# Vision tower on one core: the opening loads in another order, position tables built by the host, and a new planned order of tasks

## The chip, the cores and the metric

The kernel runs on one core of a Trainium2 chip. Its engines are TensorE (PE: matrix products and transposes), VectorE (DVE), ScalarE (ACT), GpSimd (POOL) and SyncE (SP, which here only issues transfers and waits). The metric is the device time of one execution in microseconds; it was measured in three runs.

## The reference

The input is 32 images of 3 x 96 x 96 and 31 small parameter arrays. All is fp32. In short:

```
h = patches(x) as 36 rows of 768 per image               # tokenizer
h = layernorm(h, ln1) @ W + bias;  h = layernorm(h, ln2) + sincos positions
h = [cls_tok ; cls_token + cls_pos_embedding ; h]        # 38 rows of 256 per image, 1216 rows
h += causal 16-head attention(layernorm(h)), weights quantised to 5 levels:
     s = mean|w|;  w = clip(round(w / s), -2, 2) * s
h += tanh(layernorm(h) @ weight.T @ aux1.T @ aux2 + bias)
h += 16-head attention(layernorm(h)) with biases and a head mask
h += top-1 of 16 experts(layernorm(h)), hidden size 1024, 76 rows of room for each expert
```

## The kernel before

**Tiles.** A tile is three images (TROWS = 114 rows; 11 tiles, the last of 76). The tokens are kept in `tokens` (whose first 256 columns are `h`). Attention works on pairs of images (16 per layer). The raw patches come twice: `in_xt` by token, from which VectorE takes the mean and variance of each row (task `xs`), and `in_xf` by feature, the left side of the token product (task `tok`). Both come in five groups of tiles, XGROUPS = (0,1), (1,2), (2,4), (4,7), (7,11). The normalisation of the first layer norm is folded into the weights: `cs` (on PE, L742) sums the weighted columns of W and VectorE builds `tokWg` from it (L1080); `bs` adds up the bias (L748, L1087). `asum` (L1091) sums the absolute attention weights, PE adds them over the partitions (`qs`, L755), and VectorE quantises `attn0` (`qs`, L1096 to L1108). `fB` and `fW` (L766) multiply the three weights of the feed-forward layer into one; `wo` and `bo` do the head mask and a bias of the second attention layer. A tile's product goes through VectorE (`tok`, L1125), its variance through GpSimd (L654, L655: add epsilon, power -0.5), then `tokn` (L1134, L1135) applies the second norm and adds the table `addA`. GpSimd makes `addA` at the start (L637, L638) from three tables.

**PSUM.** Products that pass through the three banks `G` are numbered in PE's order (`uses`), and use n waits until use n - 3 has been emptied by VectorE or ScalarE.

**Values.** In each attention layer the value rows of a tile are copied to three blocks of partitions by 9 transfers on SP (`sp` task `v`, L599), after which GpSimd masks them by head (`vb`, L675). GpSimd also masks the keys (`km`, L662). Once the last token tile is done, SP issues the first expert weights, one piece after each `v`. After attention the rows are scattered to the experts (L695) into `expert_in`, which was first filled from `k_empty`, and the experts run in a loop (L919, L932).

**The order.** Each engine takes its tasks strictly in the order that `plan()` (L300) works out at build time. `needs()` gives the dependences, COST the planned time of each task, ARRIVES and XARRIVES the planned landing times of loads, HANDOVER what passing a result on costs, and GOAL the wanted times. At each step an engine picks, of the next tasks of its kinds, the one with the lowest value of

```
c[0] * EAGER + wanted(*c[1][1:])
```

where c[0] is the planned start (L340). The kernel's loads are issued at the start, on SP's queue (L560 to L571) and on ScalarE's (L953 to L960), each queue in the order of its lines. ScalarE's first task, and the first `tokn`, wait for `tables_ready` (L640).

## Time and profile before

| | |
|---|---|
| median of 3 runs | 445.86 us (443.11 to 446.62) |
| profiled execution | 444.86 us |
| its span | 443.2 us |
| mean granted TensorE clock | 0.892 of full |
| PE busy | 370.4 us (84%) |
| VectorE busy | 235.5 us (53%) |
| GpSimd busy | 178.0 us (40%) |
| ScalarE busy | 113.7 us (26%) |
| moved by DMA | 64.68 MB, mean 146 GB/s |

Times inside the span are counted from the first instruction. Busy time does not hold the issue of transfers, semaphore waits or branches; a matmul of the source is two or more records, since fp32 goes through in parts. Idle time of an engine counts only where something on the chain waits for it. The DMA engines are fully busy for about the first 40 us (296 to 429 GB/s in the page's slices of 11 us) and lightly used until the expert weights.

### The profile page before, as it was taken

The page shows a single profiled execution, that of the slowest core. Times are in us where ns is not written, and L with a number is a line of the kernel's source. Part 1 is how long each engine was busy: PE and PEld are TensorE (multiplying, and loading weights), DVE is VectorE, ACT ScalarE, POOL GpSimd, SP SyncE. Part 2 cuts the span into 40 slices and gives each one's busy share as a digit, 9 for nine tenths or more (in the row PEclk, how much of TensorE's full clock was granted, in tenths as well). Part 3 has the DMA queues.
Part 4 walks back from the last instruction along what each step waited for, and adds up shares of the span by engine and source line. Part 5 has one row for each costly group of instructions (what it writes and reads, how often), then busy time and mean ns, then how long its engine had stood idle before and what let it go on. Part 6 is the DMA issues. An engine that isn't in the chain of part 4 may idle for free.

```text
span 443.2 us, 9050 instructions
## 1 busy us (share of the span) xinstructions
PE 370.4 (84%) x3164; PEld 307.6 (69%) x3164; DVE 235.5 (53%) x675; ACT 113.7 (26%) x333; POOL 178.0 (40%) x264
## 2 busy tenths in 40 slices
PE   4649998799998989887858667984499999999992
PEld 3537886687787968766747546764398888888881
DVE  1298998687887368565666474465022232222221
ACT  0001233344444445343423322211021101111010
POOL 0224566665556537344536451645011313132221
PEclk9968999899999989888997895555589999999998
DMA  8997011110122212223233323531868999999200
GB/s 296 401 429 299 23 42 33 35 46 30 34 82 91 60 55 84 87 73 88 75 105 85 112 76 103 138 124 32 211 214 275 317 317 324 315 315 324 66 16 5
DMA packets 39237, 64.68 MB, mean 146 GB/s; under 512 B 5147, under 2 KB 30684, under 8 KB 38368
## 3 DMA queue, kind: packets, MB, share of 16 engines
q1 hardware_dynamic: 32752, 53.86, 36.7%
q10 hardware_dynamic: 2208, 6.82, 4.4%
q0 software_dynamic: 4240, 3.51, 3.0%
q8 instruction: 23, 0.38, 0.3%
q14 instruction: 14, 0.11, 0.1%
HBM read 53.20 MB, written 7.62 MB: 137 GB/s over the span
## 4 chain that ended last, share of the span: by engine, by line
PE 59%; issue 12%; DMA 8%; DVE 7%; SPq 6%; POOL 5%; ACT 1%; ACTq 1%; DVEq 0%; POOLq 0%
PE bank L919 13%; PE bank L932 12%; SPq L599 6%; PE bank L782 5%; PE bank L806 5%; PE bank L867 4%; DMA early<-in_xt 4%; PE bank L853 4%; PE bank L816 3%; DMA v<-vt 3%; PE bank L842 3%; PE bank L834 2%; PE bank L874 2%; POOL mid L662 2%; PE bank L791 1%
## 5 line engine op out<-in xcount | busy, mean ns | idle before, releaser
L675 POOL TENSOR_TENSOR mid<-v,tab 114x512 f32<-114x512 f32 x32 | 34.4, 1078 | 74.8 <-DMA v<-vt 51.9
L919 PEld LDWEIGHTS bank<-mid,early 128*128 128x128 f32 x512 | 61.9, 199 | 1.2
L919 PE MATMUL bank<-mid,early 128*128 (+1 forms) x512 | 61.9, 281 | 0.0
L932 PE MATMUL bank<-early,mid 128*76 128x256 f32 x256 | 57.9, 379 | 0.0
L853 PE MATMUL bank<-mid 114*38 114x51 f32 (+3 forms) x768 | 31.7, 232 | 21.2 <-issue 18.8
L853 PEld LDWEIGHTS bank<-mid 114*38 114x38 f32 (+1 forms) x768 | 28.8, 141 | 27.3 <-issue 25.2
L932 PEld LDWEIGHTS bank<-early,mid 128*76 128x76 f32 x256 | 36.6, 147 | 15.4
L712 POOL DMA_DIRECT2D mid<-in_b x14 | 7.9, 563 | 84.0 <-DVE idx L1228 84.0
L662 POOL TENSOR_TENSOR mid<-mid,tab 128x608 f32<-128x608 f32 x32 | 38.5, 1209 | 1.9 <-PE bank L834 1.8
L655 POOL TENSOR_TENSOR rs<-rs,mhalf 114x1 f32<-114x1 f32 (+4 forms) x60 | 36.8, 613 | 5.0
L806 PE MATMUL bank<-xnT,attn 128*128 128x228 f32 (+1 forms) x192 | 38.4, 355 | 0.0
L1032 ACT ACTIVATE mid<-bank,cols 128x76 f32<-128x76 f32 x64 | 15.5, 325 | 86.2 <-PE bank L919 86.2
L1216 DVE TENSOR_SCALAR mid<-bank,cols 128x76 f32<-128x76 f32 x64 | 14.5, 289 | 42.9 <-PE bank L919 42.9
L806 PEld LDWEIGHTS bank<-xnT,attn 128*128 128x128 f32 x192 | 35.1, 197 | 1.5 <-issue 0.4
L998 ACT COPY mid<-bank 114x612 f32<-114x612 f32 x32 | 21.4, 670 | 44.1 <-PE bank L842 44.1
L782 PE MATMUL bank<-early 128*114 128x256 f32 (+1 forms) x132 | 32.1, 400 | 0.4 <-DVE fv L1169 0.4
L654 POOL TENSOR_SCALAR rs<-mv 114x1 f32<-114x1 f32 (+4 forms) x60 | 15.2, 253 | 41.5 <-DVE mv L1055 29.9
L1149 DVE TENSOR_REDUCE mx<-bank 102x16 f32<-102x608 f32 x32 | 25.0, 783 | 12.6 <-PE bank L834 12.5
L867 PE MATMUL bank<-attn,mid 128*114 128x256 f32 (+1 forms) x88 | 29.3, 464 | 0.6 <-ACT mid L1003 0.4
L1144 DVE TENSOR_SCALAR xn<-tokens,mv,rs 114x256 f32<-114x256 f32 (+1 forms) x33 | 21.0, 644 | 16.5 <-POOL rs L655 15.6
L993 ACT ACTIVATE mid<-mid 102x608 f32<-102x608 f32 x32 | 22.8, 714 | 26.2 <-DVE mid L1152 26.0
L782 PEld LDWEIGHTS bank<-early 128*114 128x114 f32 (+1 forms) x132 | 24.3, 187 | 6.7 <-DVE fv L1169 0.8
(112 smaller groups left out, 588.9 us busy)
## 6 DMA issues: line engine op xcount, KB each, us to landing
early<-in_w SPq DMA_DIRECT2D x64, 512.0 KB, 5.1
v<-vt SPq DMA_DIRECT2D x192, 38.0 KB
expert_in<-k_empty SPq DMA_DIRECT2D x1, 2570.0 KB, 37.0
attn<-in_attn SPq DMA_DIRECT2D x2, 1024.0 KB, 19.5
early<-in_xt ACTq DMA_DIRECT2D x1, 1536.0 KB, 35.9
early<-in_xf SPq DMA_DIRECT2D x1, 1368.0 KB, 20.1
mid<-expert_in SPq DMA_DIRECT2D x8, 160.6 KB, 6.6
mid<-expert_in ACTq DMA_DIRECT2D x8, 160.6 KB, 7.0
```

What stands on the lines that cost most here:

```text
L599: sp.dma_start(v3[j * SEQ:(j + 1) * SEQ, (TILE_IMGS * n + a) % (2 * TILE_IMGS), :], vt[a * SEQ:(a + 1) * SEQ, (m - 1) % 2, :]).then_inc(v_ ...
L655: eng.tensor_tensor(rs[0:r, at, :], rs[0:r, at, :], bc(mhalf[0:r, :], 1, width), ALU.pow).then_inc(rs_ready, 1)
L662: eng.tensor_tensor(km[:, n % 2], bc(kT[:, :, n * PCOLS:(n + 1) * PCOLS], 2, 4), bc(bc(quarterm[:, :], 2, PCOLS), 1, KC), ALU.mult).then_i ...
L675: eng.tensor_tensor(Vb[0:TROWS, (m - 1) % 3, :, :, 0:HD], v3[:, at:at + 2, :].rearrange("p a (h d) -> p a h d", h=HEADS), bc(bc(blockm[:, ...
L782: mm_ = mm(ps[0:rows(n), 0:DIM], xT[:, n, j, 0:rows(n)], tokWg[:, j, :], start=j == 0, stop=j == PC - 1)
L806: ins = mm(ps[:, oc * width:(oc + 1) * width], w[:, kc, j * DIM + oc * 128:j * DIM + oc * 128 + 128], xnT[:, kc, gcols(n)], start=kc == 0, ...
L853: ins = mm(Op[r0:r1, h0 * VW:h1 * VW], PTs[0:TROWS, n % 2, j, r0:r1], Vb[0:TROWS, (m - 1) % 3, a, h0:h1, :], start=True, stop=True)
L867: ins = mm(ps[0:rows(n), 0:DIM], OT[:, kc, cols(n)], w[:, kc, :], start=kc == 0, stop=kc == KC - 1)
L919: ins = mm(Hp[b][:, c // 4, (c % 4) * ECOLS:(c % 4 + 1) * ECOLS], w1s[s][:, kc, c * 128:c * 128 + 128], xeT[:, bass.ds(it * SLOTS + s, 1), ...
L932: ins = mm(Yp[b][0:CAP, 0:DIM], hT[:, b, c, :], w2s[s][:, c, :], start=c == 0, stop=c == HC - 1)
L993: eng.activation(P[0:PROWS, n % 2], P[0:PROWS, n % 2], ACT.Exp).then_inc(p_exp, 1)
L1149: link(eng.tensor_reduce(mxv, sv, AX.X, ALU.max))
```

## The change

Four things are changed.

1. The sincos positions leave the constant table `k_tab` (553 columns become 297) and are put by the host into the second half of `in_table`, which held only the class position. GpSimd makes `addA` in one addition instead of two chained ones, into a tile of its own.
2. That addition, the scaling of `bq` and the copy of the row ids are no longer GpSimd's first work but a task `tabs`, placed by the planner. The first `tokn` depends on it in the plan; the waits in the kernel are as before.
3. The loads are issued in another order. SP: W, features 0, features 1, attn0, features 2, 3, 4, ffn0, attn1. ScalarE: cols, tokens 0, table, tokens 1, live, gain, tab, tokens 2, mask, tokens 3, tokens 4, k_empty. The mask and k_empty pass from SP's queue to ScalarE's.
4. The planner's arrivals, wanted times, TILE and EAGER have new values, so the order of the tasks on all engines is planned anew. COST is the same but for the new task.

```diff
--- before.py
+++ after.py
@@ -63,7 +63,7 @@
 NEG = -1.0e30
 DROP = 65536.0
 
-TAB = {"ident": 128, "head": 8, "quarter": 4, "block": HEADS, "upto": TROWS, "iota": EXP, "ids": TILES, "pos": DIM}
+TAB = {"ident": 128, "head": 8, "quarter": 4, "block": HEADS, "upto": TROWS, "iota": EXP, "ids": TILES}
 COLS = {"g1": PC, "be1": PC, "bq": KC, "bk": KC, "bv": KC, "gate": KC * EXP, "b1": EXP * HC}
 LIVE_ROWS = ["L0_tok_bias", "L0_ffn_bias", "L1_attn_bo", "L1_ffn_bg", "L1_attn_head_mask"]
 
...
@@ -115,6 +109,16 @@
     return np.ascontiguousarray(w.reshape(-1, 128, w.shape[-1]).transpose(1, 0, 2).reshape(128, -1))
 
 
+def positions():
+
+    omega = np.arange(DIM // 4, dtype=np.float32) / np.float32(DIM // 4 - 1)
+    omega = (np.float32(1.0) / np.power(np.float32(10000.0), omega)).astype(np.float32)
+    y, x = np.meshgrid(np.arange(HP, dtype=np.float32), np.arange(HP, dtype=np.float32), indexing="ij")
+    y, x = y.reshape(-1)[:, None] * omega, x.reshape(-1)[:, None] * omega
+    one = np.concatenate([np.zeros((2, DIM), np.float32), np.concatenate([np.sin(x), np.cos(x), np.sin(y), np.cos(y)], 1)], 0)
+    return one.astype(np.float32)
+
+
...
@@ -126,11 +130,12 @@
     by_feature = tok.reshape(TILES, TROWS, PC, 128).transpose(3, 0, 2, 1)
     row = lambda names: np.concatenate([inputs[n].reshape(1, -1) for n in names], 1)
     column = lambda name, k: inputs[name].reshape(k, 128).T
-    gain, add, cls_pos = [np.zeros((XROWS, DIM), np.float32) for _ in range(3)]
+    gain, add, place = [np.zeros((XROWS, DIM), np.float32) for _ in range(3)]
     for a in range(TILE_IMGS):
         at = a * SEQ
         gain[at + 2:at + SEQ], add[at + 2:at + SEQ] = inputs["L0_tok_ln2_g"].reshape(1, -1), inputs["L0_tok_ln2_b"].reshape(1, -1)
-        add[at], add[at + 1], cls_pos[at + 1] = inputs["cls_tok"].reshape(-1), inputs["L0_tok_cls_token"].reshape(-1), inputs["L0_tok_cls_pos_embedding"].reshape(-1)
+        place[at:at + SEQ] = positions()
+        add[at], add[at + 1], place[at + 1] = inputs["cls_tok"].reshape(-1), inputs["L0_tok_cls_token"].reshape(-1), inputs["L0_tok_cls_pos_embedding"].reshape(-1)
...
@@ -145,7 +150,7 @@
         "in_cols": np.ascontiguousarray(np.concatenate([
             column("L0_tok_ln1_g", PC), column("L0_tok_ln1_b", PC), qk_bias("L1_attn_bq"), qk_bias("L1_attn_bk"), column("L1_attn_bv", KC),
             by_rows(inputs["L1_ffn_Wg"]), inputs["L1_ffn_b1"].reshape(EXP * HC, 128).T], 1)),
-        "in_live": row(LIVE_ROWS), "in_gain": gain, "in_table": np.concatenate([add, cls_pos], 1),
+        "in_live": row(LIVE_ROWS), "in_gain": gain, "in_table": np.concatenate([add, place], 1),
...
@@ -169,26 +174,26 @@
     return v.to_broadcast(shape)
 
 
-PAIR, TILE, LAYER, EAGER = 7.41, 13.22, 126.9, 529.73
-
-GOAL = {"xs": -80.1, "cs": -215.9, "bs": -113.4, "asum": -20.1, "qs": -171.8, "fB": -118.7, "fW": 6.3, "wo": 51.3, "bo": 9.8,
-        "tok": -66.3, "tokn": -11.2, "lns0": -52.5, "lnt0": -41.6, "qk0": -35.7, "v": -4.5, "km": -49.3, "s": -0.2, "vb": 8.1, "pt": 8.7,
-        "pv": 15.8, "ot": 19.9, "proj": 28.5, "lns1": -74.7, "lnt1": 31.5, "ffn": 42.8, "ffnr": 30.3, "lns2": -36.9, "lnt2": 54.0,
-        "qk1": 66.1, "lns3": 30.6, "lnt3": 40.2, "log": 20.5, "cnt": 26.2, "scat": 79.9}
+PAIR, TILE, LAYER, EAGER = 7.41, 13.24, 126.9, 895.91
+
+GOAL = {"xs": -73.3, "tabs": -83.3, "cs": -201.3, "bs": -78.2, "asum": -29.1, "qs": -145.2, "fB": -132.3, "fW": 13.9, "wo": 34.6,
+        "bo": 4.2, "tok": -74.4, "tokn": -17.7, "lns0": -61.1, "lnt0": -43.3, "qk0": -34.7, "v": -5.2, "km": -99.7, "s": 1.2, "vb": 2.0,
+        "pt": 9.6, "pv": 16.5, "ot": 19.7, "proj": 28.4, "lns1": -88.6, "lnt1": 35.0, "ffn": 42.8, "ffnr": -2.7, "lns2": -95.3,
+        "lnt2": 57.3, "qk1": 69.2, "lns3": 24.1, "lnt3": 35.0, "log": 5.3, "cnt": -2.7, "scat": 64.7}
 
...
+        "pool": {"xs": 0.95, "tabs": 1.3, "tok": 0.9, "lns": 0.9, "km": 1.33, "vb": 1.12, "lnx": 0.78, "cnt": 0.36, "scat": 1.3},
...
-ARRIVES = {("pe", "cs"): 6.0, ("pe", "bs"): 6.0, ("dve", "asum"): 10.0, ("dve", "wo"): 25.0, ("pe", "fB"): 22.0}
-
-XARRIVES = [8.5, 11.0, 15.0, 20.0, 26.0]
+ARRIVES = {("pe", "cs"): 6.2, ("pe", "bs"): 6.2, ("dve", "asum"): 14.5, ("pool", "tabs"): 13.0, ("dve", "bs"): 11.0, ("dve", "wo"): 38.0, ("pe", "fB"): 34.0}
+
+XARRIVES = [8.9, 11.5, 17.0, 22.5, 30.0]
 
...
@@ -214,6 +219,7 @@
         step("pe", kind, 0, 0)
         step(EMPTIES[kind], kind, 0, 0, ("pe", kind, 0, 0))
     step("dve", "asum", 0, 0)
+    step("pool", "tabs", 0, 0)
     step("dve", "wo", 0, 0)
     after[("pe", "qs", 0, 0)] = [("dve", "asum", 0, 0)]
     after[("pe", "fW", 0, 0)] = [("act", "fB", 0, 0)]
@@ -226,7 +232,7 @@
         step("pe", "tok", 0, t, ("dve", "cs", 0, 0))
         step("dve", "tok", 0, t, ("pe", "tok", 0, t), ("pool", "xs", 0, group), ("dve", "bs", 0, 0))
         step("pool", "tok", 0, t, ("dve", "tok", 0, t))
-        step("dve", "tokn", 0, t, ("pool", "tok", 0, t))
+        step("dve", "tokn", 0, t, ("pool", "tok", 0, t), *([] if t else [("pool", "tabs", 0, 0)]))
         for j, source in enumerate((("tokn", 0), ("proj", 0), ("ffnr", 0), ("proj", 1))):
             step("dve", "lns", j, t, ("dve",) + source + (t,))
             step("pool", "lns", j, t, ("dve", "lns", j, t))
...
@@ -452,10 +458,12 @@
         g1, be1, bq, bk, bv, gateW_, b1T = carve(cols_, COLS.values())
         gateW = gateW_.rearrange("p (k n) -> p k n", k=KC)
         tab = sb("tab", [128, sum(TAB.values())])
-        ident, headm, quarterm, blockm, upto, iota, ids, addA = carve(tab, TAB.values())
-        blockm, upto, iota, ids, addA = [v[0:TROWS, :] for v in (blockm, upto, iota, ids, addA)]
+        ident, headm, quarterm, blockm, upto, iota, ids = carve(tab, TAB.values())
+        blockm, upto, iota, ids = [v[0:TROWS, :] for v in (blockm, upto, iota, ids)]
         maskb = sb("maskb", [128, 8 * SEQ + 128], BF16)
         causb, identb = maskb[:, 0:8 * SEQ], maskb[:, 8 * SEQ:8 * SEQ + 128]
+        added = sb("added", [128, DIM])
+        addA = added[0:TROWS, :]
         ones = sb("ones", [128, 128])
         liveB = sb("liveB", [128, 3 * DIM + EXP + HEADS])
         biasB, fbB, boB, bgB, hmB = carve(liveB, [DIM] * 3 + [EXP, HEADS])
@@ -559,16 +567,13 @@
                 sp.dma_start(xT_[:, t0 * PC * TROWS:t1 * PC * TROWS], i["in_xf"][:, t0 * PC * TROWS:t1 * PC * TROWS]).then_inc(l_xf[j], 16)
             sp.dma_start(tokW.rearrange("p k n -> p (k n)"), i["in_tokw"]).then_inc(l_tokw, 16)
             by_feature(0)
+            by_feature(1)
             sp.dma_start(attn0[:, :], i["in_attn0"]).then_inc(l_attn0, 16)
-            by_feature(1)
-            by_feature(2)
-            sp.dma_start(maskb[:, :], k["k_mask"]).then_inc(l_mask, 16)
-            by_feature(3)
-            by_feature(4)
+            for j in range(2, len(XGROUPS)):
+                by_feature(j)
             sp.dma_start(temp_[:, 0:3 * KC * DIM], i["in_ffn0"]).then_inc(l_ffn0, 16)
             sp.dma_start(attn1[:, :], i["in_attn1"]).then_inc(l_attn1, 16)
 
-            sp.dma_start(xbuf.rearrange("(p r) n -> p (r n)", p=128), k["k_empty"]).then_inc(l_zero, 16)
...
@@ -631,13 +636,6 @@
             pool.wait_ge(l_cols, 16)
             eng.tensor_scalar(gs[:, :], g1, 1.0 / (PC * 128), None, ALU.mult).then_inc(gs_ready, 1)
             eng.memset(ohs[:, 0, :], 0.0)
-
-            pool.wait_ge(l_tab, 16)
-            pool.wait_ge(l_table, 16)
-            link(eng.tensor_tensor(addA, addA, table[0:TROWS, 0:DIM], ALU.add))
-            link(eng.tensor_tensor(addA, addA, table[0:TROWS, DIM:2 * DIM], ALU.add))
-            eng.tensor_scalar(bq, bq, 0.25, None, ALU.mult)
-            eng.tensor_copy(tokens[:, :, 2 * DIM:2 * DIM + 1], ids.unsqueeze(2)).then_inc(tables_ready, 1)
 
             counts = {"mv": 0, "km": 0}
             for kind, l, n in order("pool"):
@@ -653,6 +651,12 @@
                     pool.wait_ge(mv_ready, counts["mv"])
                     link(eng.tensor_scalar(rs[0:r, at, :], mv[0:r, at, 1:2], EPS, None, ALU.add))
                     eng.tensor_tensor(rs[0:r, at, :], rs[0:r, at, :], bc(mhalf[0:r, :], 1, width), ALU.pow).then_inc(rs_ready, 1)
+                elif kind == "tabs":
+                    pool.wait_ge(l_tab, 16)
+                    pool.wait_ge(l_table, 16)
+                    eng.tensor_tensor(addA, table[0:TROWS, 0:DIM], table[0:TROWS, DIM:2 * DIM], ALU.add)
+                    eng.tensor_scalar(bq, bq, 0.25, None, ALU.mult)
+                    eng.tensor_copy(tokens[:, :, 2 * DIM:2 * DIM + 1], ids.unsqueeze(2)).then_inc(tables_ready, 1)
                 elif kind == "km":
 
                     emptied(pool, uses[("qk", l, 2 * n // GROUP_IMGS)] + 1)
@@ -952,12 +956,16 @@
                 act.dma_start(xt_[:, t0 * PC * 128:t1 * PC * 128], i["in_xt"][:, t0 * PC * 128:t1 * PC * 128]).then_inc(l_xt[j], 16)
             act.dma_start(cols_[:, :], i["in_cols"]).then_inc(l_cols, 16)
             by_token(0)
+            act.dma_start(table, i["in_table"]).then_inc(l_table, 16)
+            by_token(1)
+            act.dma_start(liveB[:, :], i["in_live"].rearrange("a n -> (a n)").partition_broadcast(128)).then_inc(l_live, 16)
+            act.dma_start(gain[:, :], i["in_gain"]).then_inc(l_gain, 16)
             act.dma_start(tab[:, :], k["k_tab"]).then_inc(l_tab, 16)
-            act.dma_start(liveB[:, :], i["in_live"].rearrange("a n -> (a n)").partition_broadcast(128)).then_inc(l_live, 16)
-            act.dma_start(table, i["in_table"]).then_inc(l_table, 16)
-            act.dma_start(gain[:, :], i["in_gain"]).then_inc(l_gain, 16)
-            for j in range(1, len(XGROUPS)):
-                by_token(j)
+            by_token(2)
+            act.dma_start(maskb[:, :], k["k_mask"]).then_inc(l_mask, 16)
+            by_token(3)
+            by_token(4)
+            act.dma_start(xbuf.rearrange("(p r) n -> p (r n)", p=128), k["k_empty"]).then_inc(l_zero, 16)
 
             done = {}
             act.wait_ge(tables_ready, 1)
```

## Rows read from the trace of the kernel before

**Rows 1.** The page, chain that ended last: shares of the span by engine.
```profile
PE 59%; issue 12%; DMA 8%; DVE 7%; SPq 6%; POOL 5%; ACT 1%; ACTq 1%; DVEq 0%; POOLq 0%
```

**Rows 2.** Busy time by stretch: window, length; each engine; PEclk, DMA share, GB/s.
```profile
20.00:30.00 10.00, 4.74 (x12) 3.69 (x13) 8.11 (x20) 0.00 (x0) 2.85 (x6) 0.67 1.02 421
...
240.00:280.00 40.00, 29.09 (x329) 23.57 (x328) 22.36 (x80) 12.89 (x38) 16.30 (x21) 0.78 0.34 98
280.00:310.00 30.00, 22.25 (x130) 17.78 (x128) 18.95 (x95) 5.09 (x22) 14.76 (x24) 0.56 0.37 107
310.00:443.00 133.00, 117.82 (x800) 100.25 (x800) 31.39 (x115) 17.13 (x67) 28.28 (x33) 0.94 0.71 225
```

**Rows 3.** Opening transfers: tile, queue, count, size, us from issue to landing.
```profile
attn<-in_attn SPq DMA_DIRECT2D x1, 1024.0 KB, 9.1
tab<-k_tab ACTq DMA_DIRECT2D x1, 276.5 KB, 9.5
...
liveB<-in_live ACTq DMA_DIRECT2D x1, 400.0 KB, 11.7
...
early<-in_xf SPq DMA_DIRECT2D x1, 1026.0 KB, 15.5
early<-in_xt ACTq DMA_DIRECT2D x1, 384.0 KB, 17.3
...
early<-in_xf SPq DMA_DIRECT2D x1, 1368.0 KB, 20.1
early<-in_xt ACTq DMA_DIRECT2D x1, 768.0 KB, 21.0
...
early<-in_xt ACTq DMA_DIRECT2D x1, 1152.0 KB, 25.5
```

**Rows 4.** Timeline of the issues: start, length, queue, line, transfer, count.
```profile
1.80 0.43 SPq L562 DMA_DIRECT2D attn<-in_attn  x1
1.82 0.45 ACTq L955 DMA_DIRECT2D tab<-k_tab  x1
...
4.16 0.99 SPq L559 DMA_DIRECT2D early<-in_xf  x2
4.33 2.10 ACTq L952 DMA_DIRECT2D early<-in_xt  x4
```

**Rows 5.** Timeline of VectorE and TensorE, 14 to 46 us: start, length, work.
```profile
14.06 0.42 DVE L1087 TENSOR_TENSOR liveB<-bank,liveB 114x256 f32<-114x256 f32 x1 [0.59 <-DMA liveB<-in_live]
...
21.69 1.02 DVE L1070 BATCH_NORM_STATS2 xst<-early 114x6 f32<-114x384 f32 x2 [7.20 <-DMA early<-in_xt]
...
22.86 1.70 DVE L1091 TENSOR_REDUCE asum<-attn 128x1 f32<-128x1536 f32 x1
...
25.69 5.03 PE L782 MATMUL bank<-early 128*114 128x256 f32 x12
...
26.14 1.91 DVE L1070 BATCH_NORM_STATS2 xst<-early 114x6 f32<-114x384 f32 x4
...
31.47 1.54 DVE L1107 TENSOR_SCALAR attn<-attn,qs 128x512 f32<-128x512 f32 x3
...
33.56 3.65 PE L766 MATMUL bank<-early 128*128 128x256 f32 x8 [2.84 <-DVE tokens L1125]
...
35.07 2.83 DVE L1070 BATCH_NORM_STATS2 xst<-early 114x6 f32<-114x384 f32 x6
...
45.01 1.90 PE L766 MATMUL bank<-early 128*128 128x256 f32 x8
```

**Rows 6.** Timeline of GpSimd: the first of the two table additions.
```profile
15.93 0.72 POOL L637 TENSOR_TENSOR tab<-tab,mid 114x256 f32<-114x256 f32 x1 [9.65 <-DMA mid<-in_table]
```

**Rows 7.** Waits, 200 to 310 us (total, times, longest); one set of spread issues.
```profile
POOL mid L675 <- DMA v<-vt: 34.0, 6, 6.5
...
PE bank L853 <- issue: 15.1, 6, 5.2
...
217.84 7.45 SPq L599 DMA_DIRECT2D v<-vt  x9
```

More of the change, by code:

```diff
@@ L88, in constants @@
     iota = np.broadcast_to(np.arange(EXP, dtype=np.float32), (TROWS, EXP)).copy()
-    omega = np.arange(DIM // 4, dtype=np.float32) / np.float32(DIM // 4 - 1)
-    omega = (np.float32(1.0) / np.power(np.float32(10000.0), omega)).astype(np.float32)
-    y, x = np.meshgrid(np.arange(HP, dtype=np.float32), np.arange(HP, dtype=np.float32), indexing="ij")
-    y, x = y.reshape(-1)[:, None] * omega, x.reshape(-1)[:, None] * omega
-    one = np.concatenate([np.zeros((2, DIM), np.float32), np.concatenate([np.sin(x), np.cos(x), np.sin(y), np.cos(y)], 1)], 0)
-    pos = np.tile(one, (TILE_IMGS, 1)).astype(np.float32)
-    parts = {"ident": np.eye(128, dtype=np.float32), "head": head, "quarter": quarter, "block": block, "upto": upto, "iota": iota, "ids": ids, "pos": pos}
+    parts = {"ident": np.eye(128, dtype=np.float32), "head": head, "quarter": quarter, "block": block, "upto": upto, "iota": iota, "ids": ids}
     tab = np.zeros((128, sum(TAB.values())), np.float32)
@@ L182 @@
                 "pv": 0.74, "proj": 0.48, "ffn": 0.46, "ffnr": 0.5, "log": 1.35, "cnt": 0.95},
-        "pool": {"xs": 0.95, "tok": 0.9, "lns": 0.9, "km": 1.33, "vb": 1.12, "lnx": 0.78, "cnt": 0.36, "scat": 1.3},
+        "pool": {"xs": 0.95, "tabs": 1.3, "tok": 0.9, "lns": 0.9, "km": 1.33, "vb": 1.12, "lnx": 0.78, "cnt": 0.36, "scat": 1.3},
         "act": {"fB": 0.65, "fW": 0.65, "lnt": 0.4, "qk0": 1.15, "qk1": 1.9, "v": 0.42, "s": 0.74, "pt": 0.72, "ot": 0.5, "ffn": 0.45, "log": 0.55},
@@ L279, in wanted @@
 def wanted(kind, l, n):
-    if kind in ("cs", "bs", "asum", "qs", "fB", "fW", "wo", "bo"):
+    if kind in ("cs", "bs", "asum", "qs", "fB", "fW", "wo", "bo", "tabs"):
         return GOAL[kind]
```

## Prediction

> **What bounds the kernel now.** The profiled execution took 444.86 us, 1.66 us more than its span of 443.2, and lies between the lowest and the median of the three runs (443.11 and 445.86). I read four views. The page's chain of waits comes first: TensorE holds most of it, and "issue" and DMA most of the rest [rows 1]. The table by stretch then says where TensorE isn't full: in the opening, and in the last part of the second attention layer, 240 to 310 us, where it is busy for 29.1 of 40 and 22.3 of 30 us at granted clocks of 0.78 and 0.56. The expert stage from 310 us on takes 133 us and nothing in it is touched [rows 2]. The two landing lists and the timeline show what holds the opening.
>
> There, VectorE goes idle after the small bias step and starts the second group of token statistics at 21.69, on the landing of that group [rows 5]. The piece was issued at 4.33 and took 17.3 us: it landed at 21.6 [rows 3, 4]. Behind it on VectorE stand the weight sums (22.86), the first tile, the third group (26.14), and the quantisation, which ends at 31.47 + 1.54 = 33.0. TensorE waits for that chain twice: it does the third token tile from 25.69 for 5.03 us, and the next work starts at 33.56 [rows 5]. So the opening is bound by VectorE's order and the token landings, not by TensorE.
>
> **How the two queues share.** This decides the sum. The queues' transfers end in pairs, by position in the queue: third on each, tab (276.5 KB) at 1.82 + 9.5 = 11.3 and attn0 (1024 KB) at 1.80 + 9.1 = 10.9; seventh, the second token group (384 KB) at 21.6 and the fourth feature group (1026 KB) at 4.16 + 15.5 = 19.7; eighth, the third token group (768 KB; issued about 4.86) at 25.9 and the fifth feature group (1368 KB; about 4.66) at 24.8 [rows 3, 4]. All have 128 rows. The queues advance row for row, not byte for byte, and a queue with short rows gets few bytes.
> By this rule I add up pairs, with sizes from shapes. The first three pairs before hold 2884 KB and are in at 11.3; nine hold 10268 KB and are in at 30.9 (the fourth token group, issued about 5.4, took 25.5) [rows 3, 4]: (10268 - 2884) / 19.6 = 377 KB/us. Set against the eighth pair, 8348 KB, this gives 25.8, and 25.9 was measured.
> The Trainium skill, page "DMA: Bandwidth & Descriptors", section "Queues, rings and completion order", says that each DMA engine goes round the queue rows packet by packet and drains a whole packet before it switches. The trace agrees, in that the pairs above end together whatever their size; by that page a better order inside one queue does not help if the other queue's large rows stand opposite.
>
> **The loads, changed.** The pairs become: cols with tokw 857 KB, group 0 with group 0 726, table with features 1 598, tokens 1 with attn0 1408, live with features 2 1084, gain with features 3 1154, tab with features 4 1516, tokens 2 with ffn0 1536, mask with attn1 1132; then tokens 3, tokens 4 and k_empty alone on ScalarE's queue. Running sums, counted at 377 KB/us from 2884 KB at 11.3:
> - tokens 1: 3589 KB, 13.2 instead of 21.6;
> - live: 4673 KB, 16.0; before, VectorE used it at 14.06 just as it landed (2.3 + 11.7 = 14.0) [rows 3, 5];
> - tab: 7343 KB, 23.1 instead of 11.3;
> - tokens 2: 8880 KB, 27.2 instead of 25.9. It is still eighth in its queue, and attn0 is still opposite something ahead of it; the 128 KB of positions left out of tab are outweighed by ffn0, which is now ahead.
>
> **VectorE's order.** The planner picks by start time times EAGER plus wanted time. At 18.2 of its clock it compares the statistics of group 2 (arrival 17, so ready) with the quantisation, ready at 18.7: 0.5 x 896 = 450 against a difference in wanted times of 98 in the other direction. Group 2 stays ahead, as before. The order of the opening is then what the trace shows: group 0, cs, bs, group 1, asum, tile 0, group 2, qs, tile 1, tile 2, group 3. Timed: bs at 16.0, group 1 at about 16.5; from there to the start of group 2 before took 26.14 - 21.69 = 4.45 us [rows 5], so VectorE comes to group 2 at 21.0 and waits until 27.2 + 0.1. Before it started at 26.14 without waiting. What had been an idle time ahead of group 1 is one ahead of group 2. **Term: +1.2 us** (27.3 - 26.14), and all behind it (the quantisation, tile 1, the bank that TensorE needs) is 1.2 later: TensorE resumes at 34.8 instead of 33.56. Bounds: -5.1 (21.0 - 26.14) if tokens 2 is in by the time VectorE gets there; +2.7 if ScalarE's queue lags SP's by 1.5 us more here (in the three pairs above it lags by 0.4, 1.9 and 1.1). I take the value in between, since it is nearest to the eighth pair's own row.
>
> **Tables.** One of two 0.72 us additions on GpSimd goes [rows 6]; none was on the path. As a task it is planned at 13.0 and so stands behind the statistics of group 0 and ahead of those of group 1 and tile 0. On the chip GpSimd will sit there until tab is in, about 23. Who waits: VectorE's tile 1 needs group 1's factor, ready by about 26, and VectorE gets there at about 34, behind group 2 and the quantisation; the cover is 8 us. ScalarE also starts on this signal, and has its first work after 34. Term 0. The cover would go only if tokens 2 came in before 21 and tile 1 stood ahead of the quantisation: VectorE would be there at about 23.5, and 2.5 us would show.
>
> **Moved loads.** Tokens 3 (11163 KB) lands at about 33.3 and is read at about 36 (35.07 before, [rows 5]); tokens 4 (37.4), the mask and attn1 (30.2) are read once the first tiles are through. k_empty stands last on its new queue; its first reader is a scatter of the second layer. SP's queue is shorter by two issues, ahead of spreads that come after the opening. All 0. Were a queue alone slower by a sixth, tokens 3 would be in at 33.9: still covered; with that cover gone, each us later than 36 would be one on VectorE's chain.
>
> **The weight product fB** is planned at 34 instead of 22, so behind more tiles. It took 3.65 us from 33.56, the second product of the same size 1.90 [rows 5]; the difference is the clock (0.67 of full in the mean from 20 to 30 [rows 2], after TensorE had been idle). Whatever work comes first after the idle pays that. ffn0 is in by 27.2, so it waits for no load in either place, and it is the same work ahead of or behind a tile: a move, 0, between -1.75 and +1.75 us.
>
> **The rest of the order** is new throughout, and nothing in the diff shows its effect. The exposed place is the second layer: GpSimd waits there for the spread of values 34.0 us in 6 waits, and TensorE 15.1 us in 6, the longest 5.2 [rows 7]. A set of nine spread issues takes 7.45 us on SP's queue [rows 7] where the planner counts 5.4. Term 0, with -10 to +10 us: two of the longest waits less or more.
>
> **Sum:** 444.86 + 1.2 = 446.1; the same step from the median would give 447.1. I say **446**, by the execution whose rows I used.
>
> **Rivals.**
> A. *The opening pays.* If both queues got half the bytes, tokens 2 would need 2 x 2558 = 5115 KB in all, and be in at 11.3 + (5115 - 2884) / 377 = 17.2, before VectorE comes: -5.1, and up to 1.75 more if the work after a shorter idle time escapes the low clock that fB paid. 438.0 to 439.8. For it: asum is in fact 4 to 5 us earlier. Against it: the pairs of [rows 3, 4]; at 21.6 ScalarE's queue had landed 1918 KB, SP's at 19.7 already 4294.
> B. *The new order waits less in layer two.* One or two of the 5.2 us waits go: 446.1 - 5.2 = 440.9 to 435.7. For: 18.7 us of TensorE's idle time lies in 240 to 310 [rows 2].
> C. *The new order waits more there: slower.* "vb" is wanted earlier (2.0 instead of 8.1), so GpSimd, which takes its queue in order, stands sooner before a spread that SP has not finished, with masked keys and statistics behind it. It decides once GpSimd comes to a pair less than the 7.45 us of issues plus a landing after ScalarE has written the values. One or two further waits of 5.2: 451.3 to 456.5. For: TensorE's clock in 280 to 310 is 0.56, so lost time is made up slowly.
>
> **Chances.** A measurement of this kernel can tell about 1%, 4.5 us, from no change (441.4 to 450.3 about the median). My forecast case (opening as worked out, the rest within 4 us or so) 0.42, its own range 442 to 450; it gives 0.28 to "same", 0.07 to either side beyond. A 0.13, B 0.18, C 0.27. Faster 0.13 + 0.18 + 0.07 = 0.38, same 0.28, slower 0.27 + 0.07 = 0.34. The range 436 to 455 leaves out about 2 in 10: the far ends of B and C.
>
> **What would show it.** Right: tokens 1 lands near 13, tab near 23, tokens 2 near 27; VectorE idle some 6 us ahead of group 2 and starting it at 27.3; GpSimd's addition near 23; TensorE's second start at about 34.8; the expert stage again 133 us. Wrong: tokens 2 in before 24, or the quantisation done before 31 (then A); a quantisation ahead of group 2. The end of the attention stage against 310 minus what the opening gave says what the new order is worth (B or C).

## The result, and the profile after

The changed kernel takes 449.99 us (median of 4 runs, 448.54 to 453.19), the kernel before 444.75 us on the same chip (4 runs, 443.11 to 446.62). The ratio is 1.0138, 95% interval 1.0094 to 1.0182: slower by 1.4%. 446 was predicted (range 436 to 455), with a chance of 0.28 for "same", within 1%, and of 0.34 for "slower". Some executions of a kernel fall into a slower state, so each ratio in this document is of fast executions only, while each time is the median of all. The profiled execution took 450.74 us with a span of 449.1, 5.9 more than before; the sizes below are taken from it.

The page of the changed kernel: busy time and share of the span by engine, then the chain that ended last.

```profile
PE 368.8 (82%) x3164; PEld 304.7 (68%) x3164; DVE 231.9 (52%) x675; ACT 113.8 (25%) x333; POOL 176.3 (39%) x263
...
PE 48%; SPq 13%; issue 12%; DMA 12%; DVE 6%; POOL 5%; ACT 1%; ACTq 1%; DVEq 0%; POOLq 0%
```

No engine has more to do than before, but for 0.1 us of ScalarE: TensorE and VectorE are busy 1.6 and 3.6 us less. In the chain of what the end waits for, TensorE holds 48% instead of 59%, while the issues on SP's queue and the landings hold 25% instead of 14% [rows 1]. These shares do not tell the cost: the run with the new loads and the old order, 0.2% slower than before, has this chain:

```profile
PE 41%; SPq 16%; issue 15%; DMA 13%; POOL 7%; DVE 5%; ACT 1%; ACTq 1%; DVEq 0%; POOLq 0%
```

By stretch (window, length; PE, PEld, DVE, ACT, POOL busy; PEclk, DMA share, GB/s), still the changed kernel:

```profile
20.00:40.00 20.00, 8.65 (x29) 6.57 (x30) 13.81 (x37) 0.00 (x0) 6.04 (x15) 0.74 1.05 432
...
60.00:80.00 20.00, 14.01 (x138) 10.99 (x137) 14.87 (x32) 6.20 (x14) 11.30 (x20) 0.92 0.11 37
...
320.00:450.00 130.00, 117.59 (x800) 100.02 (x800) 31.38 (x115) 17.13 (x67) 27.00 (x30) 0.95 0.71 226
```

The window from 60 to 80 us in the kernel before:

```profile
60.00:80.00 20.00, 18.44 (x228) 15.47 (x227) 15.34 (x35) 7.79 (x18) 11.40 (x18) 1.00 0.12 38
```

The expert stage has the same 800 records and 117.6 us of TensorE (117.82, [rows 2]): nothing is lost there. From 60 to 80 us TensorE is busy for 14.0 us, against 18.4 us in the same window before: the loss is already there, ahead of layer two.

The opening transfers of the changed kernel (tile, queue, size, us from issue to landing), and then the issues of the first two (start, length, queue):

```profile
early<-in_xt ACTq DMA_DIRECT2D x1, 1536.0 KB, 29.5
...
early<-in_xt ACTq DMA_DIRECT2D x1, 1152.0 KB, 26.3
...
early<-in_ffn SPq DMA_DIRECT2D x1, 768.0 KB, 21.5
early<-in_xt ACTq DMA_DIRECT2D x1, 768.0 KB, 22.5
...
liveB<-in_live ACTq DMA_DIRECT2D x1, 400.0 KB, 13.7
...
tab<-k_tab ACTq DMA_DIRECT2D x1, 148.5 KB, 19.0
```

```profile
4.47 0.49 SPq L574 DMA_DIRECT2D early<-in_ffn  x1
4.66 0.52 ACTq L956 DMA_DIRECT2D early<-in_xt  x1
```

The third token group (tokens 2, 768 KB) was issued at 4.66 and is in at 4.66 + 22.5 = 27.2; `fB`'s weights (in_ffn) at 4.47 + 21.5 = 26.0, far ahead of the 34 that the new plan assumes.

The timeline of the changed kernel (start, length, engine, line, operation, count; in brackets the idle time before it and what ended it), VectorE and GpSimd first:

```profile
17.22 1.02 DVE L1078 BATCH_NORM_STATS2 xst<-early 114x6 f32<-114x384 f32 x2
...
23.21 0.73 POOL L657 TENSOR_TENSOR added<-mid 114x256 f32<-114x256 f32 x1 [13.15 <-DMA tab<-k_tab]
27.17 1.94 DVE L1078 BATCH_NORM_STATS2 xst<-early 114x6 f32<-114x384 f32 x4 [5.40 <-DMA early<-in_xt]
...
32.52 1.54 DVE L1115 TENSOR_SCALAR attn<-attn,qs 128x512 f32<-128x512 f32 x3
...
48.11 0.38 DVE L1152 TENSOR_SCALAR xn<-tokens,mv,rs 114x256 f32<-114x256 f32 x1
```

VectorE waits 5.40 us for tokens 2 and starts that group at 27.17 (26.14 before, [rows 5]). The last row, the first tile's rows normalised for attention, comes at 48.11; before, it came at 43.62. So 1.0 us late has become 4.5. TensorE and ScalarE show where:

```profile
34.52 10.32 PE L786 MATMUL bank<-early 128*114 128x256 f32 x36 [10.47 <-DVE tokens L1133]
...
44.68 1.89 PE L770 MATMUL bank<-early 128*128 128x256 f32 x8
46.40 2.75 PE L786 MATMUL bank<-early 128*114 128x256 f32 x12
48.99 1.89 PE L770 MATMUL bank<-early 128*128 128x256 f32 x8
50.72 0.60 PE L795 MATMUL bank<-tab,xn 114*128 114x114 f32 x4
...
52.97 0.37 ACT L998 COPY vt<-bank 114x256 f32<-114x256 f32 x1 [0.95 <-PE bank L820]
...
64.29 0.37 ACT L998 COPY vt<-bank 114x256 f32<-114x256 f32 x1 [6.81 <-DMA v<-vt]
...
166.74 0.37 ACT L998 COPY vt<-bank 76x256 f32<-76x256 f32 x1 [1.48 <-PE bank L820]
...
314.42 1.15 POOL L699 DMA_INDIRECT expert_in<-tokens,sloti  x1 [0.31 <-issue]
```

The same places in the kernel before:

```profile
37.04 7.93 PE L782 MATMUL bank<-early 128*114 128x256 f32 x36
...
43.62 0.41 DVE L1144 TENSOR_SCALAR xn<-tokens,mv,rs 114x256 f32<-114x256 f32 x1
...
44.81 0.36 PE L791 MATMUL bank<-tab,xn 114*128 114x114 f32 x2
...
47.81 0.37 ACT L990 COPY vt<-bank 114x256 f32<-114x256 f32 x1 [0.28 <-PE bank L816]
...
158.92 0.35 ACT L990 COPY vt<-bank 76x256 f32<-76x256 f32 x1
...
308.31 1.15 POOL L695 DMA_INDIRECT expert_in<-tokens,sloti  x1 [1.05 <-DVE sloti L1199]
```

TensorE resumes with three token tiles (36 records), then `fB` (8 records, 44.68), one more tile (12), `fW` (8), and only then the transposes of the first two tiles (50.72). Before, `fB` came first at 33.56 [rows 5], the three tiles at 37.04, and the first transposes at 44.81, 5.9 us earlier. The first values are written at 52.97 (47.81 before), the last tile's values of the first layer at 166.74 (158.92 before), and the last scatter to the experts is issued at 314.4 (308.3 before). A delay as large as the 5.9 us of the span is there at the first transposes and at the end; in between it isn't constant (3.8 us at the first masked scores, 7.8 at the last tile's values). One wait in the rows above is new: ScalarE writes the third tile's values only after 6.81 us of waiting for the spreads of the first ones (`v<-vt`; `vt` has two places), which were issued from 53.4 on.

### The profile page after: what moved, and what is told of

Read it like the earlier page. It is cut to its first block, busy times and chain, and to the rows that moved or that the text cites. A ratio compares the mean times of both kernels' runs of the same rounds, so it can differ in the third digit from the quotient of the medians.

```text
span 449.1 us, 9051 instructions
## 1 busy us (share of the span) xinstructions
PE 368.8 (82%) x3164; PEld 304.7 (68%) x3164; DVE 231.9 (52%) x675; ACT 113.8 (25%) x333; POOL 176.3 (39%) x263
## 4 chain that ended last, share of the span: by engine, by line
PE 48%; SPq 13%; issue 12%; DMA 12%; DVE 6%; POOL 5%; ACT 1%; ACTq 1%; DVEq 0%; POOLq 0%
PE bank L923 13%; SPq L604 13%; PE bank L936 12%; DMA v<-vt 5%; DMA early<-in_xt 5%; PE bank L857 3%; PE bank L786 3%; PE bank L871 3%; PE bank L820 3%; POOL mid L679 2%; PE bank L838 2%; PE bank L846 2%; PE bank L878 2%; DMA mid<-expert_in 1%; PE bank L810 1%
## 5 line engine op out<-in xcount | busy, mean ns | idle before, releaser
L857 PEld LDWEIGHTS bank<-mid 114*38 114x38 f32 (+1 forms) x768 | 28.9, 141 | 22.5 <-issue 20.9
L786 PE MATMUL bank<-early 128*114 128x256 f32 (+1 forms) x132 | 33.8, 415 | 10.6 <-DVE tokens L1133 10.5
L786 PEld LDWEIGHTS bank<-early 128*114 128x114 f32 (+1 forms) x132 | 25.3, 195 | 17.4 <-DVE tokens L1133 10.9
L810 PEld LDWEIGHTS bank<-xnT,attn 128*128 128x128 f32 x192 | 34.5, 195 | 1.3 <-issue 0.4
L1152 DVE TENSOR_SCALAR xn<-tokens,mv,rs 114x256 f32<-114x256 f32 (+1 forms) x33 | 20.0, 618 | 22.4 <-POOL rs L653 22.0
L1233 DVE TENSOR_TENSOR mid<-bank,mid 76x256 f32<-76x256 f32 x16 | 6.7, 421 | 39.9 <-PE bank L936 39.9
## 6 DMA issues: line engine op xcount, KB each, us to landing
early<-in_xt ACTq DMA_DIRECT2D x1, 1536.0 KB, 29.5
```

The lines of the kernel that those rows point to most:

```text
L786: mm_ = mm(ps[0:rows(n), 0:DIM], xT[:, n, j, 0:rows(n)], tokWg[:, j, :], start=j == 0, stop=j == PC - 1)
L810: ins = mm(ps[:, oc * width:(oc + 1) * width], w[:, kc, j * DIM + oc * 128:j * DIM + oc * 128 + 128], xnT[:, kc, gcols(n)], start=kc == 0, ...
L857: ins = mm(Op[r0:r1, h0 * VW:h1 * VW], PTs[0:TROWS, n % 2, j, r0:r1], Vb[0:TROWS, (m - 1) % 3, a, h0:h1, :], start=True, stop=True)
```

## The experiments

Two theories to begin with. **O**, the order: the loads cost the predicted 1 us, the planned order the rest, and that in the first tiles. **L**, the loads: all of it comes from the opening. Each run below has its ratio to the kernel before on the same chip, with the 95% interval. Three marks are read from each trace: the first values written, the first masked scores on VectorE, and the issue of the last scatter (before 47.8, 60.2, 308.3; changed 53.0, 64.0, 314.4).

### Loads and order apart

The changed kernel, with the numbers of the planner as before, wanted times and arrivals too (`tabs` as GpSimd's second task):

```diff
-PAIR, TILE, LAYER, EAGER = 7.41, 13.24, 126.9, 895.91
+PAIR, TILE, LAYER, EAGER = 7.41, 13.22, 126.9, 529.73
... (GOAL, ARRIVES, XARRIVES as before)
+    orders["pool"].insert(1, ("tabs", 0, 0))
```

> The changed kernel's loads and tables, with the order of before (GpSimd's table task second in its queue, as in the changed kernel). Theory O (the new order costs the time, the loads only 1.2 us): third token group starts at 27.2, TensorE's next work at 34.6, first values written at 49.0 (47.8 before, 53.0 changed), time 1 to 2 us above before (ratio 1.002 to 1.004). Rival L (the new loads cost it): ratio 1.010 to 1.018, like the changed kernel.

Ratio 1.0023 (1.0000 to 1.0046), 446.37 us. TensorE resumes at 34.57, first values at 50.0, last scatter at 308.6. The loads' part is +0.2%, 1.0 us. In this trace the first values are 2.2 us later than before, since `fB` took 3.75 us and the three tiles behind it 9.10 instead of 7.93, but the last scatter is only 0.3 us later: most of this delay is made up on the way.

The other half: the kernel before, with the changed kernel's planner numbers and its task `tabs` in the plan only.

```diff
-PAIR, TILE, LAYER, EAGER = 7.41, 13.22, 126.9, 529.73
+PAIR, TILE, LAYER, EAGER = 7.41, 13.24, 126.9, 895.91
... (GOAL, ARRIVES, XARRIVES as changed; tabs left out of GpSimd's order)
```

> The loads and tables of before, with the changed kernel's order. Theory O: third token group starts at 26.1, but the first transposes stand behind both weight products and a seventh token tile, so first values at 51.8, and the time 3 to 5 us above before (ratio 1.007 to 1.012). Rival L: ratio 1.00, within 1 us of before.

Ratio 1.0113 (1.0080 to 1.0145), 451.22 us; first values at 50.9, last scatter at 314.0. 1.0023 x 1.0113 = 1.0136, against 1.0138 for both: the parts add up, and the order makes 1.1 of the 1.4%. L falls.

### The first tiles

The changed kernel; only the tasks of the first two tiles and the two weight products are put back where the order of before had them:

```diff
+    orders["pe"].remove(("fB", 0, 0))
+    orders["pe"].insert(orders["pe"].index(("tok", 0, 3)), ("fB", 0, 0))
+    # abridged: so too lnt 0, fW, v 0, lnt 1 ahead of tok 6; dve: tokn 0, lns 0 ahead of tok 4,
+    # lnx 0, tokn 1, lns 1 ahead of tok 5; pool: lns 0, lns 1; act: lnt 0, v 0
```

> The changed kernel with the steps of the first two tiles in the order of before on all four engines: the first weight product ahead of the fourth token tile, the second one and the seventh tile behind the first transpose. Theory F (what costs is that the first transposes come late, and the delay is carried to the end): first values at 49, time 3 to 4 us below the changed kernel (ratio to before 1.003 to 1.006). Rival M (the order is worse in the middle, wherever it begins): first values at 49 too, but the pairs lose it again by 120 us and the ratio stays at 1.010 or more.

Ratio 1.0041 (1.0005 to 1.0076), 447.52 us: 1.0 of the 1.4% are gone, and what is left of the order, beside the loads' 0.2%, is within the uncertainty. Its first values are at 49.4, though the first masked scores come at 66.5, later than in the changed kernel, and ScalarE's third values wait 2.60 us for spreads. Its last scatter comes at 311.7: 2.8 us earlier than in the changed kernel, and 3.0 later than with the whole old order. So by the traces half of the order's delay is left, by the times next to none; a trace is one execution, and those of this kernel lie some 6 us apart. That the first tiles carry most of the order's cost rests on the times. The two halves of this edit were then tried alone.

TensorE's and ScalarE's half, the products and transposes put back:

```diff
+    orders["pe"].remove(("fB", 0, 0))
+    orders["pe"].insert(orders["pe"].index(("tok", 0, 3)), ("fB", 0, 0))
+    # and the rest of the pe and act moves above; dve and pool as in the changed kernel
```

> The changed kernel with only the two weight products, the seventh tile, the first transposes and the first values moved back on TensorE and ScalarE; VectorE's order stays the new one. Of the 4 us by which the first values come later than the loads explain, I expect VectorE's two tiles more ahead of the first normalised rows to keep about 2 (first transposes at 48.6 instead of 50.7, first values at 51 instead of 53.0) and the products to be the other 2: ratio to before 1.008 to 1.011, against 1.0138 changed and 1.0041 with all the first tiles' steps moved. If the products are all of it, 1.004.

Ratio 1.0152 (1.0108 to 1.0195), 451.99 us, first values at 55.9: a gain was expected and there is none. TensorE in this kernel:

```profile
50.10 0.61 PE L809 MATMUL bank<-tab,xn 114*128 114x114 f32 x2 [3.75 <-issue]
50.50 3.65 PE L784 MATMUL bank<-early 128*128 128x256 f32 x8
```

TensorE comes to the transposes and stands idle for 3.75 us, because VectorE, which does two more tiles first, has the rows only at 49.6; and behind the idle time the second product takes 3.65 us instead of 1.89. The other half, VectorE's and GpSimd's order put back:

```diff
+    orders["dve"].remove(("tokn", 0, 0))
+    orders["dve"].insert(orders["dve"].index(("tok", 0, 4)), ("tokn", 0, 0))
+    # and the rest of the dve and pool moves above; pe and act as in the changed kernel
```

> The other half of the run that moved the products alone: the changed kernel with VectorE's and GpSimd's first two tiles in the order of before, TensorE and ScalarE in the new one. VectorE has the first normalised rows at about 45.0 instead of 48.1, but the first transposes stand on TensorE behind the first product, the seventh tile and the second product and start at 50.7 as in the changed kernel: first values at 53, ratio 1.010 to 1.016, no gain. If VectorE's order alone is the cause, first values at 50 and 1.004.

Ratio 1.0179 (1.0124 to 1.0234), 453.24 us, first values at 53.3: no gain, as expected. From its timeline:

```profile
43.77 0.41 DVE L1166 TENSOR_SCALAR xn<-tokens,mv,rs 114x256 f32<-114x256 f32 x1
...
51.03 0.56 PE L809 MATMUL bank<-tab,xn 114*128 114x114 f32 x4
```

The rows are ready at 43.8, as before, and lie for 7 us, since TensorE has the products and a tile ahead of them. Each engine's new order is enough by itself to keep the first tile late; only both together give it back.

### What turns the plan

The planned arrival of `fB`'s load alone, in the kernel before:

```diff
-ARRIVES = {("pe", "cs"): 6.0, ("pe", "bs"): 6.0, ("dve", "asum"): 10.0, ("dve", "wo"): 25.0, ("pe", "fB"): 22.0}
+ARRIVES = {("pe", "cs"): 6.0, ("pe", "bs"): 6.0, ("dve", "asum"): 10.0, ("dve", "wo"): 25.0, ("pe", "fB"): 34.0}
```

> The kernel before with one number changed: the planned arrival of the feed-forward weights on TensorE, 34 instead of 22 (the loads, which land them at 29.5, are those of before). The plan then has both traits of the new one: three tiles ahead of the first product, and two more tiles on VectorE ahead of the first normalised rows. Theory N (this number is what makes the new order late): first values at 51 to 52 instead of 47.8 and ratio 1.006 to 1.012. Rival G (the wanted times and EAGER do it): 1.00.

Ratio 1.0284 (1.0243 to 1.0324), 457.11 us; first values at 53.6, as in the changed kernel. TensorE of this kernel:

```profile
33.63 10.54 PE L782 MATMUL bank<-early 128*114 128x256 f32 x36 [3.83 <-DVE tokens L1125]
44.00 1.89 PE L766 MATMUL bank<-early 128*128 128x256 f32 x8
```

As in the changed kernel, `fB` runs behind three tiles, because of a single number and with all loads as before. The cost is twice that of the whole change and over twice what was expected, and by this trace the first tiles are less than half of it: the first values are 5.8 us late, the last scatter, at 321.9, is 13.6. The number changes the order on every engine far beyond the first tiles (TensorE, for one, takes the eighth tile behind the scores of the third pair instead of ahead of those of the first), so this run shows how much one number can do, not what the place of `fB` costs. The reverse, in the changed kernel:

```diff
-ARRIVES = {..., ("pe", "fB"): 34.0}
+ARRIVES = {..., ("pe", "fB"): 22.0}
```

> The changed kernel with that number back at 22. Theory N: the first product goes back ahead of the fourth tile and VectorE's first tile ahead of its fifth; first values at 48.5 to 49.5 instead of 53.0. The plan behind it also differs (two more tiles stand ahead of the first queries and keys), so part may be given back: ratio 1.002 to 1.009, against 1.0138. Rival G: 1.012 or more.

Ratio 1.0121 (1.0051 to 1.0191), 451.88 us: not shown to be better than the changed kernel. The first tile is early again (first transposes at 46.1, first values at 49.9, as with the first tiles restored), but the plan now puts two more token tiles ahead of the first queries and keys, and the second tile's values come at 65.1 instead of 57.1 and the first masked scores at 70.7 instead of 64.0. So that number turns the old plan and only part of the new one; with the other new numbers a plan of much the same cost comes out even with the first tile early.

### The quantisation ahead of the wait

VectorE's 5.4 us of waiting could hold the quantisation. In the changed kernel:

```diff
+    orders["dve"].remove(("qs", 0, 0))
+    orders["dve"].insert(orders["dve"].index(("xs", 0, 2)), ("qs", 0, 0))
```

> The changed kernel with one task moved on VectorE: the quantisation ahead of the third token group's statistics. It fills the 5.4 us idle time: quantisation from 21.7 to 26.4, third group from 27.2 without further delay, second tile at 29.4 instead of 34.0, TensorE's next work at 29.9 instead of 34.5. If the opening is bound by VectorE's order (my reading): all that follows is 4.6 us earlier, ratio to before 1.001 to 1.005, unless the fourth group (in at about 32) or the seventh tile's loads hold it at about 32 to 33, then 3 us. Rival (the opening's gain is lost in the attention layers): ratio stays at 1.010 or more.

Ratio 1.0057 (1.0027 to 1.0086), 447.87 us; first values at 48.5. TensorE resumes at 29.9 instead of 34.5, and 0.8% come back. The same edit with the new loads and the old order:

```diff
+    orders["pool"].insert(1, ("tabs", 0, 0))
+    orders["dve"].remove(("qs", 0, 0))
+    orders["dve"].insert(orders["dve"].index(("xs", 0, 2)), ("qs", 0, 0))
```

> The changed kernel's loads with the order of before, and the quantisation ahead of the third token group on VectorE. If the opening shifts everything behind it (theory O): second tile at 29.4 instead of 34.0 in the run with the old order, first values at 45.5 to 46 instead of 50.0, time 3 to 5 us below that run, ratio to before 0.991 to 0.996. Rival S (the attention layers are paced by something that does not start with the first tile, such as the seven-issue-a-tile spreads on SP's queue, so that an early start is given back): ratio 1.000 or above.

Ratio 0.9938 (0.9913 to 0.9963), 441.92 us: faster than before. Against the same loads without the edit, 0.9938 / 1.0023 = 0.9915, the same 0.8%.

### Loads ordered by pairs

If the queues advance row for row, the token groups must stand early in their own queue. The planner's numbers are those of before, and GpSimd takes `tabs` behind the statistics of the fourth group. The two queues, written as lists (removed: the changed kernel's):

```diff
 # ScalarE's queue
-cols, tokens 0, table, tokens 1, live, gain, tab, tokens 2, mask, tokens 3, tokens 4, k_empty
+cols, tokens 0, live, tokens 1, tokens 2, table, tokens 3, tab, gain, mask, tokens 4, k_empty
 # SP's queue
-W, features 0, features 1, attn0, features 2, 3, 4, ffn0, attn1
+W, features 0, features 1, attn0, features 2, 3, ffn0, features 4, attn1
```

> Order of tasks of before; loads ordered by the rule of pairs: ScalarE cols, tokens 0, live, tokens 1, tokens 2, table, tokens 3, tab, gain, mask, tokens 4, k_empty; SP W, features 0, 1, attn0, features 2, 3, ffn0, features 4, attn1; GpSimd's table task behind the fourth token group. If the queues advance row for row at 377 KB/us: landings of live at 9.8, tokens 1 at 13.6, tokens 2 at 17.4 (against 27.1 in the changed kernel, with 5185 KB ahead of it instead of 8880), tokens 3 at 25.9, tab at 30.0, gain at 33.0. Third token group on VectorE starts at 19, TensorE's next work at 26.5, first values at 41 to 42 (47.8 before). Ratio to before 0.984 to 0.990 if all behind follows, 0.995 or more if it is given back (rival S). If the queues shared bytes evenly, tokens 2 would land at 15.7.

Ratio 0.9873 (0.9834 to 0.9912), 438.97 us. Landing list, issues and timeline of this kernel:

```profile
early<-in_xt ACTq DMA_DIRECT2D x1, 1152.0 KB, 21.7
...
early<-in_xt ACTq DMA_DIRECT2D x1, 768.0 KB, 14.8
```

```profile
2.30 1.32 ACTq L957 DMA_DIRECT2D early<-in_xt  x2
4.19 0.50 ACTq L957 DMA_DIRECT2D early<-in_xt  x1
...
19.55 1.91 DVE L1079 BATCH_NORM_STATS2 xst<-early 114x6 f32<-114x384 f32 x4
...
26.95 3.75 PE L771 MATMUL bank<-early 128*128 128x256 f32 x8 [4.46 <-DVE tokens L1134]
```

Tokens 2, the second of the two issues that begin at 2.30 (so at about 2.96), is in at 17.8 and tokens 3 at 4.19 + 21.7 = 25.9. The rule of pairs gave 17.4 and 25.9. An equal share of the bytes, summed as for rival A, is 2 x 2025 KB and so 14.4 for tokens 2 (the 15.7 of the expectation does not come out of that sum). VectorE starts the group at 19.55 without a wait, and TensorE resumes at 26.95 instead of 34.5. Next, the same loads and the wanted times of before, planned anew with arrivals by the rule of pairs (those of the other loads too), which puts the quantisation early:

```diff
-XARRIVES = [8.5, 11.0, 15.0, 20.0, 26.0]
+XARRIVES = [7.8, 13.6, 17.4, 25.9, 37.4]
```

> As the run with loads by pairs, planned with the arrivals of the rule of pairs and the wanted times of before; the one difference in the orders is the quantisation ahead of the third token group. Here nothing has to be filled (tokens 2 is in before VectorE comes), so it should move the second tile by nothing: within 0.5 us of the run with loads by pairs in the first values and within its interval in time.

Ratio 0.9881 (0.9841 to 0.9921), 438.41 us: no different from the last, as expected, though the first values come at 40.7 instead of 42.3. TensorE waits 4.85 us for a bank in it. Last, the quantisation also behind tile 2 and `fB` ahead of tile 5, so that banks come free early:

```diff
+    orders["dve"].remove(("qs", 0, 0))
+    orders["dve"].insert(orders["dve"].index(("xs", 0, 3)), ("qs", 0, 0))
+    orders["pe"].remove(("fB", 0, 0))
+    orders["pe"].insert(orders["pe"].index(("tok", 0, 5)), ("fB", 0, 0))
```

> The fastest so far (loads by pairs, order of before) with the quantisation behind the third tile on VectorE and the first product behind the fifth tile on TensorE. VectorE empties the banks of tiles 1 and 2 at about 22 and 24 instead of 26 and 27, so TensorE's idle time of 4.9 us before 26 and the low clock behind it go. The first normalised rows are then bound by VectorE's own work and the fourth group's landing (25.9): first values at 38.5 to 40.5 (40.7 before this edit), ratio 0.982 to 0.988. If the opening is by now bound by VectorE's busy time alone, nothing: 0.988.

Ratio 0.9814 (0.9765 to 0.9863), 436.93 us: the lowest ratio of all, 1.9% below the kernel before. TensorE in it:

```profile
21.94 5.44 PE L791 MATMUL bank<-early 128*114 128x256 f32 x24 [0.26 <-DVE tokens L1138]
27.21 1.89 PE L775 MATMUL bank<-early 128*128 128x256 f32 x8
32.14 4.53 PE L791 MATMUL bank<-early 128*114 128x256 f32 x12 [3.04 <-DVE tokens L1138]
```

The wait for a bank is 0.26 us instead of 4.85, but a later one of 3.04 stands in for much of it, and the first values come at 40.6, no earlier than in the version before. The intervals of the last two overlap; that this one is faster than the other isn't shown, and if it is, the first values are not the reason.

## Why the prediction was right in the opening and wrong in the order

**The number: inside the range, by luck.** The forecast had +1.2 us from 444.86; the medians are 5.2 us apart and the profiled executions 5.9. 450.0 lies in the range of 436 to 455 only because the term for the order, put at 0, carried -10 to +10 us, sized by waits in layer two that then did not grow. It also sits on the edge that I drew: just inside "same" by time (450.3), just outside by ratio (1.4%).

**The loads: right.** Predicted and measured landings: tokens 1 13.2 and 13.7, live 16.0 and 16.7, tab 23.1 and 23.1, tokens 2 27.2 and 27.2, mask 30.2 and 29.4, tokens 3 33.3 and 32.0, tokens 4 37.4 and 35.8. Only the tail, where ScalarE's queue is alone, came 1.3 to 1.6 us sooner than worked out, which nothing waited for.

**VectorE's order: right.** Group 2 at 27.17 (27.3), TensorE at 34.52 (34.8). The term of +1.2 us is +1.0 in the run with the loads alone (0.23% of 445), in part by luck: there the first values are 2.2 us late, and something behind them, which I had not in the sum, gives most of it back. Rival A's price was real, though not for this order of loads and not by equal shares: with the queues ordered by pairs the opening gave 1.3%, 5.6 us, as A had said (5.1 to 6.9).

**Tables: right.** GpSimd's addition came at 23.21; its first reader on VectorE comes after 43, so nothing waited for it.

**"A move, 0": the step that failed.** I wrote of `fB` that it is the same work ahead of or behind a tile. The part on the clock held: the work that comes first after the idle time pays (the 36 records took 10.32 us instead of 7.93, `fB` 1.89 instead of 3.65), and in the run with the loads alone the tiles behind it paid too (9.10). What it left out is who stands behind. Before, `fB` ran while VectorE was still working its way to the first normalised rows. Moved behind three tiles, and with `fW` and a fourth tile, it stands between those rows and TensorE; and VectorE, in its turn, does two more tiles ahead of them. The work is the same, but the first transposes come 5.9 us later, and what I should have followed was that tile and not the sum of work. `fB`'s place alone isn't what costs: with the products put back and VectorE's order left new the ratio was 1.0152. The step that failed is the reading of each move by its own work, on either engine.

**"The rest of the order, 0, -10 to +10": mis-sized.** The order as a whole is worth +1.1%, 5.0 us, and 1.0% of the 1.4% comes back with the first tiles. What carries the delay to the end is open. One reading is that every later stage is behind the first tiles by its dependences and that TensorE, 82% busy, has little slack to catch up in; another that the spreads on SP's queue pass it on (6.81 us of waiting for them at the third values). No run isolates either. With the order of before, the last scatter follows the first values: shifts against the kernel before of -3.5, -5.5, -7.1 and -7.2 us at the first values (quantise first, pairs, pairs and quantise first, quantise after tile 2) are -5.0, -4.2, -7.4 and -7.3 at the last scatter. The loads alone are the exception: +2.2 became +0.3. So a gain at the first values was kept, within 1.5 us, and a small loss was not. Across different orders the first values alone don't tell the time: with arrival 22 in the changed kernel they came at 49.9 (yet +1.2%), with arrival 34 in the kernel before at 53.6 (+2.8%), in the changed kernel at 53.0 (+1.4%).

**Rival C: the right sign in the wrong place.** It looked for longer waits in layer two. The waits of the changed kernel from 200 to 320 us (engine, tile, line, what was waited for; total, times, longest):

```profile
POOL mid L679 <- DMA v<-vt: 23.9, 6, 5.9
...
PE bank L857 <- issue: 15.0, 5, 5.4
```

They are 10.1 us shorter and the same (34.0 and 15.1, [rows 7]), and the last tile's values of the first layer are already 7.8 us late. So the sign that C gave came true, and its reason did not.

**Open.** Which of the other new planner numbers, beside the arrival of 34, keep the first tiles late in the new plan, and whether the rest of that plan costs anything: 1.0041 with the first tiles restored against 1.0023 with the whole old order is no difference that these runs can tell, and they would not tell one of up to about 0.6% either. The 3.0 us between their last scatters says that there may be one. The two readings of what carries the delay are open too.

## What to carry to other kernels

When an order is planned anew, don't add up the work that moves: follow the first tiles through every engine, and ask what now stands between their inputs and the first results that all later stages need. The first tile alone is not enough, as the run with arrival 22 shows. A planned arrival later than the real landing is not a safe setting: it moves work behind other work. Here it was 34 for 26.0; in the kernel before, where the same load lands at about 29.5, the 34 alone cost 2.8%. When two queues load together, as here with rows over 128 partitions on both, list their transfers in pairs by position before ordering them.

## What the runs showed of the hardware that I had not expected

The rule of pairs predicts a new order of loads well: within 1 us for live (10.8, predicted 9.8), tokens 1 (14.1, 13.6), tokens 2 (17.8, 17.4), tokens 3 (25.9, 25.9), tab (29.5, 30.0) and gain (32.1, 33.0) in the run by pairs. The same 768 KB, issued 1.7 us apart, took 22.5 us eighth in the queue and 14.8 us fifth.

Idle time of TensorE has a price after it, which moves to whatever comes next: the same 8 records took 3.56 to 3.75 us behind 2.8 to 10.6 us of idle time, and 1.89 to 1.90 us in the middle of work. For this product longer idle time did not cost more; the 36 records behind it took between 7.93 and 9.10 us. The granted clock was 0.50 of full, 1.2 GHz, from 50.5 to 54.2 in the run with the products alone, where such a product ran behind idle time, and 1.00, 2.4 GHz, from 45 to 47 in the kernel before, where one ran in the middle of work. Behind 1.2 to 2.6 us of idle time ahead of the weight sums and tile 2, the 12 records of tile 2 took 2.82 us in seven runs and 4.43 in one (the quantisation ahead of the wait, granted clock 0.63), so a short idle time is not always free. In the run with the products alone an idle time of 3.75 us was followed by such a product, so it cost about 5.5 us in all (3.75 and 3.65 - 1.89; an estimate).
